# One opening program for a two-layer decoder kernel on one Trainium2 core: row statistics and input transposes between the weight jobs, Mamba step sizes from unnormalised tiles

## The reference, cut to what matters

```python
xn = (x - mean(x)) / sqrt(var(x) + 1e-5)          # per token
zxbcdt = einsum('bld,ed->ble', xn, in_proj_w)
dt = zxbcdt[..., D_INNER + CONV_DIM:]             # 8 heads, so 8 rows of in_proj_w
dt = softplus(dt + dt_bias)
A = -exp(A_log)
decay = exp(A * dt)                               # in the scan over the 128 tokens
```

## Time and profile before

| | us |
|---|---|
| median of 3 runs (lowest, highest) | 3587.94 (3587.37, 3589.06) |
| the profiled execution, its own time | 3584.76 |
| its span in the trace | 3583.0 |
| phase `consts` | 0 to 59.98 |
| phase `steps`, first and last instruction | 60.86 to 173.84 |
| `layer0`, first DVE instruction | 176.84 |

### The profile page before, as it was taken

How to read it: one execution, slowest core, us unless ns; L and a number is a source line. 1 busy time by engine, 2 the same in 40 slices (tenths; PEclk the granted TensorE clock), 3 DMA queues, 4 the chain that set the end, 5 groups by cost and what they waited for, 6 DMA issues and landing times. The chain is left out here.

```text
span 3583.0 us, 96256 instructions
## 1 busy us (share of the span) xinstructions
PE 3146.4 (88%) x27084; PEld 2719.7 (76%) x27085; DVE 2789.4 (78%) x8803; ACT 2286.2 (64%) x8301; POOL 1522.1 (42%) x5101
## 2 busy tenths in 40 slices
PE   2869999999999999999997588888888888599998
PEld 1857888888888888888886477777777777378898
DVE  4368888888888888888883477777777787588676
ACT  1247777777777777777774477777777777133333
POOL 0024544544544544545442255555554554024233
PEclk8579999999999999999998699999999999599999
DMA  5000010000100100100000800000000000122443
GB/s 159 8 24 27 28 34 26 29 32 26 35 27 26 35 26 26 35 26 28 34 27 18 297 16 18 15 18 15 18 16 16 18 15 14 46 79 107 139 136 92
DMA packets 95515, 162.07 MB, mean 45 GB/s; under 512 B 16435, under 2 KB 61136, under 8 KB 95440
## 3 DMA queue, kind: packets, MB, share of 16 engines
q1 hardware_dynamic: 73728, 102.32, 9.5%
q0 software_dynamic: 17616, 58.02, 4.4%
q10 hardware_dynamic: 4096, 0.83, 0.1%
HBM read 102.85 MB, written 61.79 MB: 46 GB/s over the span
## 5 line engine op out<-in xcount | busy, mean ns | idle before, releaser
L381 POOL TENSOR_TENSOR tiny<-tiny 128x1 f32<-128x1 f32 x3456 | 772.1, 223 | 838.1 <-DVE tiny L368 597.3
L728 ACT ACTIVATE work<-bank,att 128x128 f32<-128x128 f32 x2048 | 720.3, 377 | 88.3 <-DVE att L718 82.8
L718 DVE TENSOR_REDUCE att<-bank 128x4 f32<-128x512 f32 x512 | 335.3, 686 | 145.5 <-PE bank L711 138.4
L728 ACT ACTIVATION_READ_ACCUMULATOR work<-bank,att 128x1 f32 x2048 | 445.3, 217 | 0.0
L209 PE MATMUL bank<-work,w0p 128*128 128x128 f32 x3072 | 429.7, 280 | 3.5 <-ACT r_tfi_ L1094 1.7
L209 PEld LDWEIGHTS bank<-work,w0p 128*128 128x128 f32 x3072 | 385.0, 195 | 12.3 <-ACT work L1019 2.6
L189 PE MATMUL bank<-w1r,workr 128*128 (+3 forms) x1058 | 361.0, 341 | 17.1 <-DVE workr L1795 16.7
L747 PE MATMUL bank<-const,work 128*128 128x128 f32 x2048 | 316.8, 278 | 51.6 <-ACT work L753 34.5
L1193 DVE SCALAR_TENSOR_TENSOR work<-work,small 128x127 f32<-128x127 f32 (+2 forms) x1152 | 318.9, 346 | 16.2 <-ACT work L1033 11.6
L191 PE MATMUL bank<-w1r,workr 128*128 (+3 forms) x1058 | 322.6, 305 | 0.0
L190 PE MATMUL bank<-w1r,workr 128*128 (+3 forms) x1058 | 322.5, 305 | 0.0
(11 more groups left out here) (307 smaller groups left out, 7786.1 us busy)
## 6 DMA issues: line engine op xcount, KB each, us to landing
work<-decay_sums SPq DMA_DIRECT2D x64, 512.0 KB, 3.6
pair_rows<-work POOLq DMA_DIRECT2D x4, 5934.0 KB, 44.8
work<-pair_rows SPq DMA_DIRECT2D x91, 258.0 KB
work<-in_ctx SPq DMA_DIRECT2D x128, 128.0 KB, 2.0
x_res<-in_x POOLq DMA_DIRECT2D x8, 1024.0 KB, 21.3
recurrence_out<-r_xo_ SPq DMA_DIRECT2D x64, 128.0 KB, 1.7
work<-recurrence_out SPq DMA_DIRECT2D x64, 128.0 KB, 2.0
out_dram<-work POOLq DMA_INDIRECT x91
```

The lines of the kernel that those rows point to most:

```text
L381: e.tensor_tensor(out_, a_, b_, ALU.add if b_ is three_halves else ALU.mult)\
L718: e.tensor_reduce(a_nm[:, 4 * g:4 * g + 4], sc_banks[g % 2][:, :].rearrange("p (h k) -> p h k", k=P), AX.X, ALU.max, negate=True).then_inc ...
L728: last = e.activation(Pb[g % 2][:, c * P:c * P + P], sc_banks[g % 2][:, c * P:c * P + P], ACT.Exp, bias=a_nm[:, 4 * g + c:4 * g + c + 1], ...
```

## The change

The two phases become one, `start`. Its parts:

- **Order of jobs.** The two `out_proj` jobs, the only ones that are scaled by `nw_row`, move from places 10 and 11 to the end of the table (32 and 33).
- **Transfers.** SP issues `dt_stage` right behind the constant table and before the weights. The other 15 small transfers move from ACT to POOL, behind the eight of x. ACT issues none.
- **Pairs.** The tiles are taken in 32 pairs (b and b + 4 of a chunk of eight), one pair per weight job. PE's order for pair p: four transposes of unnormalised x into bank 5 or 6 (`turn`, two pairs in flight), the transposes of weight job p, and the step-size matmuls of pair p - 1 (`steps`). ACT copies the pair's 512 columns (`take`) and then the first part of job p. DVE does two `bn_stats` and then the second part of job p.
- **Step sizes.** The 8 columns of dt's weights are now the stationary operand, in a block of 32 columns that is zero elsewhere (`q_w`), and the transposed tile of 128 columns moves. The output goes to 32 partitions of bank 4, which of the four groups of 32 depends on the tile; four tiles add up in one group. The two tiles of a pair fall into two different groups.
- **Correction.** After the loop ACT copies the bank (512 columns), PE turns it by four transposes, and DVE subtracts mean x (sum of weights), then multiplies by rstd, on all 512 columns at once. The weights' sums come from one product with ones.
- **The rest.** The chain up to min(v, -v), then the vector scalings that stood at the head of DVE's program, the two `out_proj` jobs, and the exp/ln chain as before. The loop `norm` and the copies of 128 x 256 are gone, and so is one barrier.

```diff
+            def turn(p):
+                if p % 4 == 0: e.wait_ge(S[f"x_loaded{p // 4}"], 16)
+                if past(p - 1): e.wait_ge(S["q_xT"], p - 1)
+                for t, b in enumerate(pair_of(p)):
+                    for c in range(2):
+                        last = e.transpose(x_bank[p % 2][:, (2 * t + c) * P:(2 * t + c) * P + P],
+                                           x_res[:, b * D + c * P:b * D + c * P + P], ident)
+                last.then_inc(S["q_tr"], 1)
+            def steps(p):
+                if p == 0: e.wait_ge(S["q_wdt"], 1)
+                e.wait_ge(S["q_xT"], p + 1)
+                for c in range(2):
+                    for t, b in enumerate(pair_of(p)):
+                        g, j = b % 16 // 4, b % 4
+                        last = e.matmul(dt_bank[32 * g:32 * g + 32, b // 16 * P:b // 16 * P + P], q_w[:, j, c, :],
+                                        q_x[p % 4][:, t, c, :], start=j == 0 and c == 0, stop=j == 3 and c == 1)
+                last.then_inc(S["q_dt"], 1)
...
+            for p in range(PAIRS_OF_X):
+                turn(p)
+                w0[1](e, [p])
+                if p > 0:
+                    steps(p - 1)
+            steps(PAIRS_OF_X - 1)
...
+            def take(p):
+                e.wait_ge(S["q_tr"], p + 1)
+                if past(p - 3): e.wait_ge(S["q_dt"], p - 3)
+                e.activation(q_x[p % 4].rearrange("p t c i -> p (t c i)"), x_bank[p % 2][:, :], ACT.Copy)\
+                    .then_inc(S["q_xT"], 1)
+            for p in range(PAIRS_OF_X):
+                take(p)
+                w0[2](e, [p])
+            e.wait_ge(S["q_dt"], PAIRS_OF_X)
+            e.activation(q_dtT, dt_bank[:, :], ACT.Copy).then_inc(S["q_held"], 1)
...
+            for p in range(PAIRS_OF_X):
+                if p % 4 == 0: e.wait_ge(S[f"x_loaded{p // 4}"], 16)
+                for b in pair_of(p):
+                    e.bn_stats(stats0[:, b, :], x_res[:, b * D:(b + 1) * D])
+                w0[3](e, [p])
...
-            def norm(b, k):
-                if past(b - 3): e.wait_ge(S["p_tr"], b - 3)
-                e.tensor_scalar(pxn[k], x_res[:, ds(b * D, D)], tab[:, ds(b * TAB + 3 * NH, 1)],
-                                tab[:, ds(b * TAB + 3 * NH + 1, 1)], ALU.subtract, ALU.mult)\
...
+            link(e.tensor_tensor(heads_of(ex), of_tiles(mean_all), small_bank[:, 0:NH].unsqueeze(1).to_broadcast([P, NB, NH]),
+                                 ALU.mult))
+            e.wait_ge(S["q_dtT"], 1)
+            link(e.tensor_tensor(v, turned_bank[:, :], ex, ALU.subtract))
+            link(e.tensor_tensor(heads_of(v), heads_of(v), of_tiles(rstd_all), ALU.mult))
+            e.wait_ge(S["small_loaded"], 15 * 16)
+            link(e.tensor_tensor(heads_of(v), heads_of(v), dtb.unsqueeze(1).to_broadcast([P, NB, NH]), ALU.add))
```

More of the change, by code:

```diff
@@ L303, in sync, with tensor @@
                     e.dma_start(stages[j % STAGES][:, 0:n], rows_).then_inc(S[f"{pre}_load{j % STAGES}"], 16)
-            def tensor(e):
-                scaled = 0
-                for j, (_, n, _, _, sc) in enumerate(jobs):
+            def tensor(e, js=None):
+                for j in js or range(len(jobs)):
+                    _, n, _, _, sc = jobs[j]
+                    scaled = sum(job[4] is not None for job in jobs[:j])
                     e.wait_ge(S[f"{pre}_load{j % STAGES}"], 16 * (j // STAGES + 1))
@@ L316, in tensor, with scalar @@
                     last.then_inc(S[pre + "_tr"], 1)
-            def scalar(e):
-                for j, (_, n, dst, f, _) in enumerate(jobs):
+            def scalar(e, js=None):
+                for j in js or range(len(jobs)):
+                    _, n, dst, f, _ = jobs[j]
                     e.wait_ge(S[pre + "_tr"], j + 1)
@@ L324, in scalar, with vector @@
                         .then_inc(S[pre + "_hi"], 1)
-            def vector(e):
+            def vector(e, js=None):
+                js = js or range(len(jobs))
                 def scale(j):
@@ L434, in decoder @@
                           (wu[r * P:(r + 1) * P, :], D, plain(w_ru, g * D + r * P), 0.5, None)]
+        jobs0 += [(out_proj[r * P:(r + 1) * P, :], DI, to(w_out, r * P), 1.0, nw_row) for r in range(2)]
         w0 = weights("w0", stage0, jobs0)
@@ L438, in decoder, with heads_of, pair_of @@
         CHUNK = max(1, NB // 8)
-        with phase("consts") as block:
+        stats0 = work[:, 1024:1024 + NB * 6].rearrange("p (b n) -> p b n", n=6)
+        pn = work[:, 1408:1408 + 4 * NB].rearrange("p (k b) -> p k b", k=4)
+        q_w = work[:, 1664:1664 + 8 * 32].rearrange("p (j c n) -> p j c n", j=4, c=2)
+        q_x = [work[:, 6144 + 512 * k:6656 + 512 * k].rearrange("p (t c i) -> p t c i", t=2, c=2) for k in range(4)]
+        pdt = [work[:, 8192 + 512 * k:8704 + 512 * k] for k in range(4)]
+        cumT = work[:, 10240:10752]
+        q_dtT = work[:, 10752:11264]
+        mean_all, rstd_all = tab3[:, :, 3 * NH], tab3[:, :, 3 * NH + 1]
+        dt_bank, turned_bank, small_bank = bank[4], bank[5], bank[7]
+        x_bank = [bank[5], bank[6]]
+        PAIRS_OF_X = NB // 2
+        def heads_of(a):
+            return a.rearrange("p (b h) -> p b h", h=NH)
+        def pair_of(p):
+            first = p // 4 * CHUNK + p % 4
+            return first, first + 4
+        with phase("start") as block:
             @block.sync
@@ L451, in _ @@
                                 x[c * CHUNK:(c + 1) * CHUNK].rearrange("b t d -> t b d")).then_inc(S[f"x_loaded{c}"], 16)
[L453 to L473, removed]
                 for dst, src in ((cw, conv_w.rearrange("(j p) o k -> p j (o k)", p=P)),
@@ L638, in _ @@
[L638 to L655 removed]
+                e.tensor_copy(tab3[:, :, NH:2 * NH], heads_of(dt_bank[:, 0:NT]))
```

192 lines of the change are left out of this document (78 added, 114 removed).

## The result

| | before | after |
|---|---|---|
| median (lowest, highest), runs | 3588.5 (3587.37, 3592.56), 4 | 3505.88 (3502.66, 3505.98), 4 |
| ratio to before, 95% interval | | 0.9766 [0.9749, 0.9783] |
| profiled execution, its span | 3584.76, 3583.0 | 3505.98, 3504.2 |
| `layer0`, first DVE instruction | 176.84 | 88.00 |
| from there to the end of the span | 3406.2 | 3416.2 |

The kernel became 82.6 us faster (by the medians), 9 us less than forecast, and inside the range. The last two lines divide this: the opening gave 88.8 us, and behind it, where no instruction was changed, 10 us came back in the profiled execution.

What follows compares the result with a forecast made beforehand. The opening was taken as a sum of stages, each bound by something else. T 59.0 plus tail 26.6 starts `layer0` at 85.6 instead of 176.84, 91.2 less: 3493.5, plus 3.2 to the median, 3497 us; range 3488 to 3532.

Steps and rivals of the forecast that it cites:

- PE per pair: Opening loop: transposes 0.68, matmuls 0.47 and mode boundaries 0.2 sum to 1.35 us per pair (1.15 to 1.87).
- 4 us later: Opening loop: the delay of T if every one of 64 tiling switches cost the upper bound of 0.16 us.
- T: Time when PE has turned the loop's last job: weights set the pace to 37.4, then 16 pairs x 1.35; 59.0 us.
- afterwards loads are no limit: Opening loop after about 37.4 us: weight transfers no longer hold PE, since 30 jobs earlier passed within 20 us.
- with 14 us to spare: Small transfers behind x on POOL's queue: landed by 51.6, needed at 66 us, so hidden.
- The tail: From T to layer0's start: Newton, 512-column steps, scalings, out_proj jobs, exp and ln, then the old end; 26.6 us.
- after 176.84 us the change alters no instruction: Behind the opening: all gain lies before layer0's first instruction, whose start moves to 85.6, 91.2 us less.
- PE at the low level: Rival, opening loop: PE stays at the slow clock, 2.45 to 3.24 us per pair, total 3528 to 3554; chance 0.20.
- The groups that don't overlap: Rival, step-size matmuls: column groups run one after another, 1.75 to 1.87 us per pair, 3503 to 3513; chance 0.20.
- Small vectors late for DVE: Rival, DVE's bias step: it waits for small transfers landing 10 to 20 us late, 3507 to 3517; chance 0.03.
- Lockstep: Rival, opening loop: each pair passes PE, ACT and DVE one after another, 5.4 us, total 3623, slower; chance 0.02.
- The change did what it says: Denies the rival that PE waits for x chunk by chunk without overlap of weights, 3543; chance 0.03.

Runs made afterwards that it cites:

- onegroup: Changed kernel with neighbouring tiles b and b + 1 as a pair, so all eight matmul rows use the same 32 columns; 3503.75 us.
- small_late: Changed kernel with POOL issuing the 15 small transfers only after 22 weight jobs are turned; 3493.99 us.
- the delays: Three runs: changed kernel plus 9, 13 or 17 unread DVE memsets at the end of the opening; 3503.30, 3512.64 and 3503.62 us.
- weights_first: Changed kernel with all 32 weight jobs ahead of the first pair on PE, ACT and DVE; 3523.53 us.
- small_on_act: Changed kernel with the 15 small transfers back on ACT's queue, ahead of its copies; 3500.94 us.

## Why the prediction was right, point by point

- **The first pairs.** x's first chunk was taken at 12.1 from transfers that ran beside ACT's; alone with the weights it released PE at 8.58. It changed nothing in the end, as the weights set the pace: job 15, forecast for 37.4, was turned at 36.37.
- **PE per pair: 1.35 forecast, 1.37 measured.** The matmuls' interval, taken from attention's row groups as 0.059, was 0.051, so they took 0.06 us less than forecast; the boundaries, put at 0.2, cost 0.28, so 0.08 more. That the two nearly cancel is luck. `onegroup` gives the bound above that the rival would have needed (0.113, 1.80). On these changes the Trainium skill (TensorEngine Tiling, Key Properties) said that a change of mode drains the engine; the earlier trace rows showed no gap, and the middle was taken. The 0.09 and 0.15 us of the trace agree with the Trainium skill in kind, and are smaller than the prediction's bound above (0.16 each). But a semaphore wait stands at each boundary too, also at the one without a change (0.04), and no run separates the two. The prediction's "4 us later" counts all 64 changes; by its own sum PE sets the pace in the last 16 pairs only, which makes it 2.
- **T: 59.0 forecast, 61.4 measured.** The step that failed is "afterwards loads are no limit", together with "POOL has no other work there" and the small vectors that are hidden "with 14 us to spare". They were hidden from DVE, which needed them at 68.75 and had them by 45 us (the last was issued at 17.6, and none took more than 26.6 to land); they were not hidden from the weights, which shared the engines with them from 34 to 44 us. The cover was checked for the one who waits for them and not for the one they travel beside. `small_late` measures that term: 3.2 us. The other deviations nearly cancel: job 15 came 1.0 early and 16 pairs took 0.3 more, so 58.3 without the packets, and `small_late` has 58.2.
- **The tail: 26.6 forecast, 88.00 - 61.36 = 26.6 measured.** Counted from T: Newton 5.1 (66.54, so 5.2), four steps on 512 columns 8.0 (8.1), min 9.2 (9.3), scalings 10.2 (10.2), the `out_proj` jobs 13.6 (13.6), exp and ln 16.5 (16.3), the old end 10.1 (10.3). All its durations had a row before, and the order of ACT's program told that exp would stand behind the copies.
- **The opening: 85.6 forecast, 88.0 measured,** and its whole difference is T's.
- **The total: 3497 forecast, 3505.9 measured.** 2.4 us are T's. The other 6.5 come from the second step that failed, the one that the whole sum rests on, "after 176.84 us the change alters no instruction: what it can win lies ahead of the first instruction of `layer0`", closed with "a changed time after `layer0` has begun, which nothing here forecasts". No instruction changed, and the time did. The profiled execution before had one of the shortest rests of the study (3406.2); after, one of the longest (3416.2). Of these 10.0 us the forecast had 3.2 in it, as the distance from that execution to the median. 5.9 of the 10 fall into the first 300 DVE instructions, with the granted clock of the third window at 0.75 in place of 0.96; the cause of that is open. With the start 5 to 9 us later and the same program behind it, the delays have rests from 3404.9 to 3418.3. So the total stands as near to the forecast as it does partly by luck: single executions of one kernel lie up to 13 us apart.
- **The rivals.** PE at the low level fell: L504's median is 273 ns, L314's pair 0.38. The Trainium skill (TensorE: Matmul & The Clock Gate, Part 4) would have led there for a loop that is mostly transposes. Two stretches of nothing but transposes disagree with it: in the earlier trace rows they reached 272 ns, and in `weights_first` they went from 421 to 273 ns at 50 us, before PE had done anything else. What differs from the 0.69 per pair of its first 43 us is that PE then stood idle between pairs and from 44.6 us on hardly did. The groups that don't overlap fell by `onegroup`. Small vectors late for DVE fell in the trace (L628 has no wait). Lockstep fell: pairs follow at PE's own sum (1.37). The change did what it says.

## What to carry to other kernels

When a transfer is moved to where its reader has time, ask also which transfers it then travels beside: the 15 small vectors were more than 20 us early for DVE and cost PE 3 us through the weights. A stage that is made of durations which all have a row can be summed to a few tenths of a microsecond, if every engine's own order is read; the time behind it, at the same instructions, still moves by several microseconds when only its start is shifted. So an edit worth a few microseconds ahead of a long program is judged by the start of the next phase in the trace, not by the median: `onegroup` and `small_on_act` lost 6 us in the one and nothing in the other.

## What the runs showed of the hardware

- Float32 matmuls of 128 columns that use two groups of 32 columns in turn come every 0.051 us at the high level, in one group every 0.113. At a boundary between full and 32-column use 0.09 to 0.15 us are lost, at one without such a change 0.04; a semaphore wait stands at each.
- The granted clock of a window can read 1.00 while PE's durations are those of the low level (two transposes 0.63 to 0.69 us): until 14 us in the changed kernel, until 49.7 us in `weights_first`. Durations tell the level.
- Transposes alone can bring PE to the high level: 421 to 273 ns at 50 us in `weights_first`, where PE had done nothing else since 6 us.
- The same instructions behind the opening took from 3404.9 to 3418.3 us in the profiled executions. The first 300 of DVE took 143.8 to 152.7 us of it, in three groups that go with the granted clock in the third 40 us (0.96, 0.86, 0.74 to 0.79); the rest of the difference was not taken apart. The delays shifted the start and left the program behind it as it was; that one kernel of them took both ways says that the instant isn't all of it. The kernel before scatters by as much between executions (3579.21 to 3593.09 in the runs beside the experiments).
- Tiny packets take the DMA engines' time without bytes: a share of 1.40 at 130 GB/s, against 1.08 at 338 without them.
